# One PSUM bank moved from the ring of row maxima to the scores of the attention

## The reference, cut to what matters

```
attn = jnp.einsum('gqd,gkd->gqk', q, k) * norm      # 32 heads, 2048 x 2048 scores each
attn = jax.nn.softmax(attn, axis=-1)
ctx  = jnp.einsum('gqk,gkd->gqd', attn, v)
```

## Time and profile before

| | |
|---|---|
| time, median of 3 runs | 3214.16 us (3214.0 to 3216.69) |
| time of the profiled execution | 3215.54 us |
| its span, first to last instruction | 3213.8 us |
| PE matmul busy | 3122.0 us, 97% |
| DVE busy | 1870.1 us, 58% |
| ACT busy | 1515.0 us, 47% |
| POOL busy | 1388.9 us, 43% |
| mean granted clock of TensorE | 0.978 |
| attention stage | from about 389 us to about 1985 us |

### The profile page before, as it was taken

One profiled execution on the slowest core, in us unless ns is written; L12 is line 12 of the kernel. 1 busy time (PEld: TensorE's weight loads), 2 busy tenths in 40 slices (PEclk: granted clock), 3 DMA queues, 4 the chain that ended last, 5 costly groups with the idle time before them and its releaser, 6 DMA issues. The chain is left out here.

```text
span 3213.8 us, 41582 instructions
## 1 busy us (share of the span) xinstructions
PE 3122.0 (97%) x15620; PEld 2117.8 (66%) x15620; DVE 1870.1 (58%) x3184; ACT 1515.0 (47%) x2852; POOL 1388.9 (43%) x480
## 2 busy tenths in 40 slices
PE   6999799999999999999999997979999999999998
PEld 5877555555555555555555543758888888888887
DVE  4444488888888888888888861743323323233232
ACT  3333156676666666666666673542222222222221
POOL 2222068888888888888888880000000000000000
PEclk8999789999999999999999999989999999999999
DMA  6665548888888888888888872752212112121111
GB/s 231 192 194 170 154 93 168 181 183 180 178 182 184 177 181 183 178 180 183 181 177 184 181 160 83 247 188 89 88 41 72 47 59 73 33 70 45 59 59 33
DMA packets 148631, 445.34 MB, mean 139 GB/s; under 512 B 26833, under 2 KB 44497, under 8 KB 113362
## 3 DMA queue, kind: packets, MB, share of 16 engines
q0 software_dynamic: 28448, 203.44, 31.3%
q1 hardware_dynamic: 118930, 239.25, 25.2%
q10 hardware_dynamic: 1056, 0.00, 0.0%
HBM read 166.85 MB, written 80.21 MB: 77 GB/s over the span
## 5 line engine op out<-in xcount | busy, mean ns | idle before, releaser
L1074 DVE TENSOR_REDUCE mxp<-pmax 128x1 f32<-128x512 f32 x2048 | 1250.9, 680 | 255.1 <-PE pmax L895 255.1
L1036 ACT ACTIVATE prob<-pexp 128x512 f32<-128x512 f32 x2048 | 1031.4, 627 | 451.2 <-PE pexp L940 448.9
L895 PE MATMUL pmax<-kst,qst 96*128 96x512 f32 x2048 | 857.0, 426 | 18.6 <-DMA v<-v_scratch 16.1
L940 PE MATMUL pexp<-qst,kst 98*128 98x512 f32 x2048 | 819.0, 402 | 3.1 <-ACT prob L1036 3.1
L895 PEld LDWEIGHTS pmax<-kst,qst 96*128 96x128 f32 x2048 | 397.2, 194 | 320.1 <-DVE mxp L1074 166.1
L1159 POOL TENSOR_TENSOR gsum<-gsum,prob 128x2048 f32<-128x2048 f32 x124 | 569.2, 4590 | 35.7 <-ACT prob L1036 24.7
L949 PE MATMUL pctx<-prob,v 128*32 128x512 f32 x4096 | 494.0, 598 | 0.0
L1159 POOL TENSOR_TENSOR gsum<-prob 128x2048 f32<-128x2048 f32 x93 | 444.6, 4781 | 87.4 <-ACT prob L1036 87.4
L940 PEld LDWEIGHTS pexp<-qst,kst 98*128 98x128 f32 x2048 | 385.9, 189 | 138.3 <-ACT prob L1036 22.2
L1667 DVE TENSOR_TENSOR hid<-sil,pl 128x512 f32<-128x512 f32 x128 | 88.0, 687 | 639.2 <-PE pl L51 631.8
L51 PE MATMUL pg<-h2f,w 128*128 128x512 f32 x1536 | 371.4, 391 | 1.0 <-issue 1.0
(11 more groups left out here) (119 smaller groups left out, 1784.0 us busy)
## 6 DMA issues: line engine op xcount, KB each, us to landing
gsum<-prob POOLq DMA_DIRECT2D x186, 1024.0 KB, 7.5
w<-w_scratch SPq DMA_DIRECT2D x128, 256.0 KB, 2.6
qst<-q_scratch SPq DMA_DIRECT2D x96, 256.0 KB, 4.6
kst<-k_scratch SPq DMA_DIRECT2D x96, 256.0 KB, 6.3
xin<-in_L_attn_query_dram SPq DMA_DIRECT2D x16, 1024.0 KB, 8.8
q_scratch<-obq SPq DMA_DIRECT2D x32, 512.0 KB, 5.0
k_scratch<-obq SPq DMA_DIRECT2D x32, 512.0 KB, 3.7
v_scratch<-vst SPq DMA_DIRECT2D x8, 1024.0 KB, 5.6
```

What stands on the lines that cost most here:

```text
L895: pe.matmul(pmax[:, bank, :], qst[0:KR, slot, qt * P:(qt + 1) * P], kst[0:KR, slot, kc * TOK:(kc + 1) * TOK], start=True, stop=True).then_ ...
L940: pe.matmul(pexp[:, score_bank(g, n), :], kst[:, slot_of(g), kt * P:(kt + 1) * P], qst[:, slot_of(g), j * TOK:(j + 1) * TOK], start=True, ...
L1036: act.activation(prob_tile(g, kt)[:, j * TOK:(j + 1) * TOK], pexp[:, score_bank(g, n), :], ACT.Exp, scale=SCALE).then_inc(exp_done, 1)
L1074: dve.tensor_reduce(mxp[:, par, u // QJ, u % QJ:u % QJ + 1], pmax[:, bank, :], X, ALU.max).then_inc(mx_done, 1)
```

## The change

The ring of maxima has three banks in place of four, and the scores have four in place of three. Nothing else changes but the banks that the first 16 maxima use and wait for: they were given out as u % MR, and are now those of the last 16 places of the ring, so that the run-in meets the ring where it begins. The order of instructions on every engine is the same as before; what differs is the bank that each of these instructions names, and the value of the semaphore that an M, a q, the transpose's bank and the sum's bank wait for.

```diff
-    MR, ER = 4, 3
+    MR, ER = 3, 4
...
+        def early_bank(u):
+
+            return ring_bank(NM - EARLY + u)
+
...
                 for u in range(EARLY):
-                    if u >= MR:
-                        pe.wait_ge(mx_done, u - MR + 1)
-                    maximum(0, 0, u, u % MR)
+                    same = [w for w in range(u) if early_bank(w) == early_bank(u)]
+                    if same:
+                        pe.wait_ge(mx_done, same[-1] + 1)
+                    maximum(0, 0, u, early_bank(u))
...
                 for u in range(EARLY):
-                    reduce(u + 1, u, 0, u % MR)
+                    reduce(u + 1, u, 0, early_bank(u))
```

## The result

| | before | changed |
|---|---|---|
| median | 3214.98 us (4 runs) | 3479.48 us (4 runs, 3474.83 to 3482.52) |
| profiled span | 3213.8 us | 3475.2 us |
| mean granted clock of TensorE | 0.978 | 0.954 |

The ratio is 1.0819 (95% interval 1.0806 to 1.0833): 8.2% slower, where 2.9% (3307 us) was forecast. The sign was right, the size was not: the medians are 264.5 us apart and the spans of the profiled executions 261, against a forecast of 93.

The account below looks back on a forecast made before the run. PE was taken to bound the attention. Later M's (+97.8 us), the fourth score bank (-4.9) and the run-in (+0.3) made +93.2 on the profiled 3215.54 us; that execution being 1.4 above the median, the forecast was 3307.4 us, range 3290 to 3330.

Parts of the forecast that it names:

- PE bounds; a block gets longer by what M7 waits: Attention blocks: M7 waits for r4, not r3; +0.345 us in ordinary blocks, +0.525 in block 4, +0.59 in block 6.
- The scores' bank, -4.9: Fourth score bank: gains nothing beside maxima, 0.49 us in each of ten blocks without maxima, -4.9 us in all.
- r0 to r7 keep their times, and the delay doesn't feed on itself: DVE in an ordinary block: late M's don't starve its reduces, so M7's +0.345 us doesn't grow from block to block.
- The clock rival: Attention: PE pauses of 0.1 to 0.35 us in each block lower the clock once a head; +55, 3362 us; chance 0.1.
- The range: Whole kernel: 3290 to 3330 us, holding the forecast, the larger stall and the edge of the smaller one.

Follow-up runs that it names:

- e2: Changed kernel with the VectorE product that divides a head's context placed before the reduce of maximum 32 in place of maximum 8: 3317.3 us, 1.0308.
- e4: Changed kernel with each GpSimd add of 2048 columns cut into four instructions of 512 columns, one signal behind the last: 3316.5 us, 1.0303.
- e5: Changed kernel with the product that divides a head's context replaced by a max-reduce of the same 512 columns, one SBUF input: 3317.9 us, 1.0315.
- e6: Changed kernel with the first GpSimd add of each head replaced by a fill of the same 2048 columns, which reads nothing: 3315.3 us, 1.0307.
- e7: e2 with three banks for the scores in place of four, three for maxima, one left unused: 3322.6 us, 1.0334.
- e11: Changed kernel with 15 spare score matmuls in front of M3 of block 1 in heads 3 to 30: 3436.3 us, 1.0673.
- e1: Changed kernel with the VectorE product that divides a head's context taking one column in place of 512: 3472.1 us, 1.0791.

## Why the prediction was wrong, point by point

- **PE bounds; a block gets longer by what M7 waits: right.** Blocks grew by 0.39; 0.345 was forecast. M7's load is 3.67 us behind M0's where the sum gave 3.65, and the way from its stream to the next M0 is 0.02 to 0.03 longer. A free head is 51.9 us for 51.6. Without the held product the banks cost 3.1% (`e2`, `e4`, `e5`, `e6`) for a forecast of 2.9%; each of these runs lies inside 3290 to 3330.
- **The scores' bank, -4.9: right** (ACT's blocks in `e7`). The rows 9 lie one block later than they are headed, in block 0 of the last head, and the rows 11 in its block 1; block 7 of head 30 has the same waits of 0.30, so the count stands.
- **"r0 to r7 keep their times, and the delay doesn't feed on itself": right for the ring, wrong as a statement on DVE.** This is the step that failed. I checked DVE's queue for starving and for order, and took the product at its 0.68 us, because every row of the kernel before had that but one: the first product behind the last maxima, at 1907.19, has 3.32 us, ends 0.56 behind an add, and I passed over it. I never asked what a delay of 0.4 us a block does to the *phase* between DVE, which follows the late M's, and GpSimd, which follows ACT. It moved the product from 0.71 to 0.47 us ahead of the add, across a boundary at 0.49. A term that the sum had at nothing, a longer product, cost 6.15 us in each of 26 heads: 26 x 6.15 = 160 us. The banks cost 98 (span of `e2`), and 98 + 160 = 258 of the 261 between the spans.
- **The clock rival: right in its mechanism, wrong in its trigger.** The clock fell once a head, but behind a stop of 4.4 us, not from pauses of 0.3: in `e2` a load for an M waited for a reduce 1085 times between 425 and 1900 us, at a granted clock of 1.00. The forecast had set beside this rival what the Trainium skill says of brief idling ("TensorE: Matmul & The Clock Gate", section "A second HAM failure mode: psum-queue depth-cycling"); the section gives no length of pause, and these pauses brought no swing. The lower clock cost 1.75 x 26 = 46 us in the changed kernel; 55 was the price.
- **The range** had no case for a new collision between engines that the change doesn't touch.

What stays open: why two heads came out 0.51 and 1.79 us ahead in the changed kernel (in the kernel before they are further ahead than most as well, 0.76 and 2.02 us), and at which moment the add takes hold. In ns, the longest lead of a held product is 0.489 us (the changed kernel) and the shortest of a free one 0.492 (`e11`, twice; `e1` has one at 0.494), over all runs that have a product and an add at this place; but the records of GpSimd are rough. Adds that are short, at a lead where a long one holds, weren't tried.

## What to carry to other kernels

From what these runs fit, size a ring by two tests: the reader's round trip over the number of banks against its own pace (does the delay feed on itself?), and how far the writer runs ahead in one burst (what does the end of a burst wait?). Then, for each delay that you accept, list the VectorE instructions with two SBUF inputs and the GpSimd instructions that read SBUF, and lay their starts beside each other: margins there are tenths of a microsecond, and a kernel with a margin of 0.2 us is one small edit away from losing 5%. Put such an instruction where the pause of its engine covers the time for which it can be held: in `e2` it started 2.2 us before the end of an add, was held until then, and cost nothing.

## What the runs showed of the hardware that was not expected

- A VectorE product of one column, 0.15 us, took 5.3 us beside a GpSimd add whose record began 0.44 to 0.48 us after it. By the records it started first and yet was the one held.
- A VectorE instruction with one input in SBUF and one in PSUM took its 0.28 us in the middle of an add, 31 times of 31.
- A GpSimd fill of 128 x 2048 fp32 took 2.10 us and held nothing; the add of the same size took 4.8.
- A stop of TensorE of 4.4 us brought the granted clock from 2.4 to 1.2 GHz; with 15 spare matmuls in it, the clock stayed at 2.4.
